# Post-norm spiking block and expert layer, one core: row sums from the producing instructions and squared deviations on ScalarE for two of the four norms

## The reference

```python
R, K, V = x @ Wr.T, x @ Wk.T, x @ Wv.T
# per time step:
r, k, v = lif(R_t), lif(K_t), lif(V_t)
h = h * 0.9 + k * v
y = r * h
x1 = layernorm(x + y @ Wo.T) * ln1_g + ln1_b
h2 = lif(x1 @ W1.T + b1) @ W2.T + b2
a  = layernorm(x1 + lif(h2)) * ln2_g + ln2_b
x3 = layernorm(x + a)                      # third norm, no gain or shift
# expert layer: softmax gates of 8 experts, the two largest, renormalised
out = layernorm(x3 + sum_e gate_e * (x3 @ We_e + be_e))   # last norm
```

## Time and profile before

| | |
|---|---|
| median of 3 runs | 991.33 us (990.92 to 992.54) |
| the profiled execution | 988.63 us, span of its core 986.8 us |
| mean granted clock of TensorE in it | 0.982 of full speed |
| PE busy, VectorE busy, ScalarE busy, GpSimd busy | 94%, 93%, 62%, 58% of the span |

### The profile page before, as it was taken

One profiled execution on the slowest core, in us unless ns is written; L12 is line 12 of the kernel. 1 busy time (PEld: TensorE's weight loads), 2 busy tenths in 40 slices (PEclk: granted clock), 3 DMA queues, 4 the chain that ended last, 5 costly groups with the idle time before them and its releaser, 6 DMA issues.

```text
span 986.8 us, 20602 instructions
## 1 busy us (share of the span) xinstructions
PE 925.7 (94%) x6506; PEld 859.1 (87%) x6506; DVE 915.6 (93%) x3682; ACT 611.8 (62%) x1389; POOL 571.8 (58%) x731
## 2 busy tenths in 40 slices
PE   5678789999999999999999999999999999999985
PEld 5578688999999999999999999999999999888764
DVE  6489998999999999999999999999999999988975
ACT  4565546666666676666666766667667666556452
POOL 1221113667676666666766666677766666765552
PEclk8799999999999999999999999999999999999999
DMA  8552222555554456555554555655545665456763
GB/s 259 129 108 66 42 54 55 118 119 118 108 112 107 100 122 119 119 122 107 114 107 99 119 118 120 127 111 104 113 97 114 119 127 110 97 97 118 141 127 86
DMA packets 59437, 109.71 MB, mean 111 GB/s; under 512 B 6592, under 2 KB 6592, under 8 KB 59328
## 3 DMA queue, kind: packets, MB, share of 16 engines
q0 software_dynamic: 37728, 68.71, 40.6%
q1 hardware_dynamic: 16992, 31.30, 9.7%
q10 hardware_dynamic: 4608, 8.39, 2.2%
HBM read 31.29 MB, written 8.39 MB: 40 GB/s over the span
## 4 chain that ended last, share of the span: by engine, by line
PE 73%; DVE 15%; ACT 3%; issue 3%; DMA 3%; POOL 2%; SPq 0%; POOLq 0%; ACTq 0%; DVEq 0%
PE ps_e L401 28%; PE ps_proj L401 12%; PE ps_proj L491 10%; PE ps_proj L476 10%; PE ps_proj L497 5%; PE ps_attn L401 3%; DVE U L887 3%; DVE V L894 2%; PE ps_zx L455 2%; DVE stats L966 2%; PE ps_attn L455 1%; DVE h L936 1%; DMA xt<-x_hi 1%; DMA xt<-x_T 1%; DMA acc<-term 1%
## 5 line engine op out<-in xcount | busy, mean ns | idle before, releaser
L887 DVE SCALAR_TENSOR_TENSOR U<-V,U 128x256 f32<-128x256 f32 (+4 forms) x576 | 227.7, 395 | 6.6 <-ACT U L658 2.9
L401 PE MATMUL ps_e<-we_hi,x_hi 128*128 128x512 f32 (+2 forms) x640 | 228.6, 357 | 3.6 <-DVE acc L1109 1.9
L894 DVE SCALAR_TENSOR_TENSOR V<-U 128x256 f32<-128x256 f32 (+4 forms) x576 | 224.2, 389 | 1.6
L401 PE MATMUL ps_e<-we_lo,x_hi 128*128 128x512 f32 (+2 forms) x640 | 223.3, 349 | 0.0
L401 PE MATMUL ps_e<-we_hi,x_lo 128*128 128x512 f32 (+2 forms) x640 | 222.7, 348 | 0.0
L1331 POOL TENSOR_SCALAR s<-U 128x256 fp32r<-128x256 f32 x208 | 192.1, 971 | 16.3 <-DVE V L894 16.3
L1317 POOL TENSOR_SCALAR veps<-mv 128x2 f32<-128x2 f32 x128 | 50.6, 396 | 256.6 <-DVE mv L972 254.4
L697 ACT ACTIVATE term<-ps_e,gate 128x256 f32<-128x256 f32 x372 | 160.3, 475 | 43.3 <-PE ps_e L401 43.3
L658 ACT ACTIVATE U<-ps_proj,cst 128x256 f32<-128x256 f32 x320 | 135.4, 480 | 70.5 <-PE ps_proj L497 64.1
L491 PE MATMUL ps_proj<-x_hi,w_hi 128*128 128x256 f32 x512 | 134.9, 284 | 3.1 <-ACT x_hi L676 1.7
L643 ACT ACTIVATE U<-ps_proj 128x512 f32<-128x512 f32 x96 | 57.6, 600 | 127.2 <-PE ps_proj L401 127.2
(11 more groups left out here) (108 smaller groups left out, 2302.3 us busy)
## 6 DMA issues: line engine op xcount, KB each, us to landing
acc<-term POOLq DMA_DIRECT2D x93, 256.0 KB, 3.7
odd_sum<-term POOLq DMA_DIRECT2D x93, 256.0 KB, 3.3
xt<-x_T SPq DMA_DIRECT2D x33, 256.0 KB, 2.9
xa<-x_tok SPq DMA_DIRECT2D x32, 256.0 KB, 3.2
xt<-x_hi POOLq DMA_DIRECT2D x32, 256.0 KB, 4.3
xb<-cst SPq DMA_DIRECT2D x32, 256.0 KB, 2.3
xb<-x_tok POOLq DMA_DIRECT2D x32, 256.0 KB, 6.1
out<-res ACTq DMA_DIRECT2D x31, 256.0 KB, 2.0
```

Of the source, the lines that this page charges most:

```text
L401: mm = pe.matmul(dst, lhs, rhs, start=(i == 0), stop=(i == n - 1))
L887: v.scalar_tensor_tensor(out=U[:, s, t, c0:c1], in0=V[:, c0:c1], scalar=0.5, in1=U[:, s, t, c0:c1], op0=ALU.mult, op1=ALU.add).then_inc(do ...
L894: v.scalar_tensor_tensor(out=V[:, c0:c1], in0=u, scalar=THRESHOLD, in1=u, op0=ALU.is_lt, op1=ALU.mult).then_inc(done, 1)
```

## The change

Norms 0 and 1 stay as they are. For norms 2 and 3 the instructions that make the norm's input also write its row sums (`accum_out`); the residual sum becomes two instructions, one for each tile. GpSimd turns the sums into minus the mean; ScalarE computes Square(x - mean) with its row sum, the result itself going to a tile that is free at that time; GpSimd makes variance + EPS and rstd of it; VectorE's shift is minus_mean * rstd. bn_stats and bn_aggr of both norms are gone, the slots of the shifts are unchanged.

```diff
@@ fin and norm counters
-        Y_STEPS, LN1_STEPS, LN2_STEPS, LN3_STEPS, GATE_STEPS, FIN_STEPS = 2, 6, 8, 5, 15, 7
+        Y_STEPS, LN1_STEPS, LN2_STEPS, LN3_STEPS, GATE_STEPS, FIN_STEPS = 2, 6, 8, 1, 15, 4
@@ ScalarE
+            def square(ln, src, junk):
+
+                for j in range(TILES):
+                    last = nc.scalar.activation(junk[:, j, :], src[:, j, :], ACT.Square, bias=minus_mean[ln][:, j:j + 1],
+                                                accum_out=squares[ln][:, j:j + 1])
+                last.then_inc(squares_ready[ln], 1)
+
+            def square_x3(b):
+                act.wait_ge(mean_ready[2], b.value(1, LAG_Z, 1))
+
+                if b.has(LAG_Y):
+                    act.wait_ge(x1T_done, b.value(1, LAG_Y, 1))
+                square(2, w, x1n)
+
+            def square_res(b):
+                act.wait_ge(mean_ready[3], b.value(1, LAG_F, 1))
+                square(3, res_of(b), odd_sum[:, b.slot(LAG_F, 2)])
...
                     for f in (0, 1):
                         to_lif(b, fill + f, COL_H1 + 2 * f * B, 2, C_B1 + 2 * f)
+                        if f == 0 and b.has(LAG_Z) and not b.early:
+                            square_x3(b)
...
                     to_lif(b, fill + 3, COL_H1 + 6 * B, 2, C_B1 + 6)
+                if b.has(LAG_F) and not b.late:
+                    square_res(b)
...
                             read_x3(b)
+                        if part == 5 and b.has(LAG_F) and b.late:
+                            square_res(b)
@@ VectorE
+                if ln in minus_mean:
+                    v.tensor_tensor(shift[ln][:], minus_mean[ln][:], rstd[ln][:], ALU.mult).then_inc(steps, 1)
+                    return
...
                 v.scalar_tensor_tensor(out=w[:, j, :], in0=w[:, j, :], scalar=rstd[1][:, j:j + 1],
-                                       in1=xb[:, j, :], op0=ALU.mult, op1=ALU.add).then_inc(ln2_steps, 1)
+                                       in1=xb[:, j, :], op0=ALU.mult, op1=ALU.add,
+                                       accum_out=sums[2][:, j:j + 1]).then_inc(ln2_steps, 1)
...
+                def total(other):
+
+                    for j in range(TILES):
+                        v.scalar_tensor_tensor(out=res_of(b)[:, j, :], in0=acc[:, b.slot(LAG_F, 2), j, :], scalar=1.0,
+                                               in1=other[:, j, :], op0=ALU.mult, op1=ALU.add,
+                                               accum_out=sums[3][:, j:j + 1]).then_inc(fin_steps, 1 + (j == 0 and b.k == LAST_BEAT))
...
-                    v.tensor_tensor(res[:], acc[:, b.slot(LAG_F, 2)], odd_sum[:, b.slot(LAG_F, 2)],
-                                    ALU.add).then_inc(fin_steps, 1)
-                if step == 2:
-                    chain(2)
-                    for j in range(TILES):
-                        bn_stats(3, j, res_of(b)[:, j, :], fin_steps)
-                if step == 3:
-                    if b.k == LAST_BEAT:
-                        dve.wait_ge(res_ready, b.value(1, LAG_F))
-                    bn_aggr(b, 3, fin_steps, FIN_STEPS, LAG_F, 4)
+                    total(odd_sum[:, b.slot(LAG_F, 2)])
...
-                    if slot == at["ln3_stats"]:
-                        after(ln2_steps, LN2_STEPS, LAG_Z, b, 8)
-                        bn_stats(2, 0, w[:, 0, :], ln3_steps)
-                        bn_stats(2, 1, w[:, 1, :], ln3_steps)
-                    if slot == at["ln3_aggr"]:
-                        bn_aggr(b, 2, ln3_steps, LN3_STEPS, LAG_Z, 2)
@@ GpSimd
+            def deviation(b, ln, steps, per, lag, done):
+
+                pool.wait_ge(steps, b.value(per, lag, done))
+                g.tensor_scalar(minus_mean[ln][:], sums[ln][:], -1.0 / D, None, ALU.mult).then_inc(mean_ready[ln], 1)
+                pool.wait_ge(squares_ready[ln], b.value(1, lag, 1))
+                g.tensor_scalar(veps[ln][:], squares[ln][:], 1.0 / D, EPS, ALU.mult, ALU.add).then_inc(rstd_ready[ln], 1)
+                pool.wait_ge(rstd_ready[ln], b.value(2, lag, 1))
+                g.tensor_tensor(rstd[ln][:], veps[ln][:], neg_half[:], ALU.pow).then_inc(rstd_ready[ln], 1)
...
-                    reciprocal_std(b, 2, ln3_steps, LN3_STEPS, LAG_Z, 4)
+                    deviation(b, 2, ln2_steps, LN2_STEPS, LAG_Z, LN2_STEPS)
...
-                    reciprocal_std(b, 3, fin_steps, FIN_STEPS, LAG_F, 6)
+                    deviation(b, 3, fin_steps, FIN_STEPS, LAG_F, FIN_STEPS - 1)
```

More of the change, by code:

```diff
@@ L246, in build @@
         gate_T = sb("gate_T", [STACK, TILES, P], F32R)
-        stats = [sb(f"stats{i}", [P, TILES, 6]) for i in range(4)]
-        mv = [sb(f"mv{i}", [P, TILES, 2]) for i in range(4)]
+        stats = [sb(f"stats{i}", [P, TILES, 6]) for i in range(2)]
+        mv = [sb(f"mv{i}", [P, TILES, 2]) for i in range(2)]
+        sums, minus_mean, squares = ({i: sb(f"{name}{i}", [P, TILES]) for i in (2, 3)} for name in ("sums", "minus_mean", "squares"))
         veps = [sb(f"veps{i}", [P, TILES]) for i in range(4)]
@@ L285, in build @@
         rstd_ready = [sem(f"rstd_ready{i}") for i in range(4)]
+        mean_ready, squares_ready = ({i: sem(f"{name}{i}") for i in (2, 3)} for name in ("mean_ready", "squares_ready"))
         e0_done, expert_done = sem("e0_done"), sem("expert_done")
@@ L791, in beat @@
                 if b.has(LAG_Z) and b.early:
-                    norm_x3(b)
+                    square_x3(b)
                 if b.ahead:
@@ L801, in beat @@
                     fill += 1
+                if b.has(LAG_Z) and b.early:
+                    norm_x3(b)
                 if b.has(LAG_Y) and not b.early:
@@ L817, in beat @@
                     read_x3(b)
+                if b.has(LAG_Z) and b.late:
+                    square_x3(b)
                 if b.has(LAG_M) and not b.early and not b.last_m:
@@ L857, in beat @@
                             read_x3(b)
+                        if part == 5 and b.has(LAG_F) and b.late:
+                            square_res(b)
+                if b.has(LAG_F) and (b.last_m or b.k == LAST_BEAT):
+                    square_res(b)
                 if b.has(LAG_F):
@@ L1116, in fin_stage @@
             def fin_stage(b, step):
-                chain = lambda n: after(fin_steps, FIN_STEPS, LAG_F, b, n)
                 if step == 0 and b.k == LAST_BEAT:
                     return
+                def total(other):
[3 more added lines that the diff above has]
+                                               accum_out=sums[3][:, j:j + 1]).then_inc(fin_steps, 1 + (j == 0 and b.k == LAST_BEAT))
                 if step == 1 and b.k == LAST_BEAT:
@@ L1122, in fin_stage @@
                     dve.wait_ge(term_ready, b.value(E - 1, LAG_F, E - 1))
-                    v.tensor_tensor(res_of(b)[:], acc[:, b.slot(LAG_F, 2)], bias_bank(b.k - 1)[:], ALU.add).then_inc(fin_steps, 2)
+                    total(bias_bank(b.k - 1))
                     return
```

## The result

The changed kernel takes **1032.97 us** (median of 4 runs, 1031.04 to 1035.13), the one before 991.31 (990.92 to 992.54): ratio 1.042, 95% interval 1.040 to 1.044. The profiled execution took 1032.87 us with a span of 1031.0, before 988.63 and 986.8. So 44.2 us of span have to be found.

What follows compares the result with a forecast made beforehand. PE was taken to set the steady beat, VectorE following with about half a microsecond of slack. 31.5 us steady plus 8 us drain, 39.5, on 991.33 gave 1030.5 us; range 1000 to 1050, the forecast's own 1012 to 1052.

Steps and rivals of the forecast that it cites:

- steady term: Steady beats: VectorE's wait for the shift makes each of 25 beats 1.26 us longer, 31.5 us in all.
- signs in the steady stretch: If right: PE 4 to 5% below 100%, VectorE near 90%, two shift waits of 1 to 2.5 us, x1_low not waiting.
- second rival: Slower by PE's banks alone: ScalarE reads late, PE waits 0.67 us per beat at an expert fill; 998 to 1012; chance 0.17.
- S, a pair of squares: ScalarE's two Square instructions with accumulator, 128x256 from SBUF: 0.99 us per pair, bounds 0.72 and 1.37.
- The accumulators on VectorE: VectorE's residual sum as two instructions, 0.79 us instead of 0.60, and 0.06 for each of four accumulator outputs.
- The new chain: Steady beats: GpSimd's operations and VectorE's last shift follow ScalarE's squares; shift 1.59 us later, beat 1.26 us longer.
- The fill: Two filling beats with a third norm: VectorE's 0.8 us partly spent in waits; 0 taken, bounds -1.5 and +1.
- The drain: Four drain beats: later shift, z_sum and x3 chain cost 1 to 2.8 us each; 8 us taken, bounds 3 and 11.
- The first rival: Faster: VectorE's wait doesn't come, PE keeps 28.06 us beats, less VectorE work shows only at the ends; 988.8 us; chance 0.15.
- The third rival: Much slower: one Square with accumulator near 1 us, a pair 1.9, loop 3.1 longer per beat; 1079 us; chance 0.08.

Runs made afterwards that it cites:

- e2: Kernel before, plus ScalarE's four squares in the steady beats at the change's places, results unused: 1012.7 us, ratio 1.022.
- e11: The changed kernel with GpSimd, in the drain's late beats, issuing two adding transfers ahead of its wait for the last norm's squares: 1028.1 us, ratio 1.035.
- e7: The changed kernel without ScalarE's squares, 1.0 standing in for both variances; sums, means, powers and shifts stay: 987.7 us, ratio 0.9945.
- e5: The changed kernel with VectorE's last-norm shift two slots later in steady beats, behind x3_low (slot 31 instead of 29): 1029.6 us, ratio 1.038.
- e9: e1 with GpSimd's issue of one transfer moved, in steady beats, between its veps and rstd of the last norm: 1031.3 us, ratio 1.039.
- e12: Kernel before, plus four idle squares per steady beat in front of ScalarE's third projection read, where it waited for PE anyway: 992.2 us, ratio 1.000.
- e1: The changed kernel with both norms' shifts made by GpSimd right behind its rstd instead of by VectorE: 1060.8 us, ratio 1.070.
- e6: e5 with ScalarE's last-norm squares moved, in steady beats, behind its read of x3 instead of ahead of expert part 3: 1056.8 us, ratio 1.064.

## Why the prediction was right, and where its sizes were off

**Direction, time and range held**: 1030.5 forecast, 1032.97 measured. That the time came so close is in part luck: the steady term was 6 us too large, the drain's 9.5 too small. Of its signs in the steady stretch, VectorE's two waits and the place of PE's (an expert fill) came as written, and x1_low waits no more. That PE's waits sit at the expert fills only it had named as a sign for its second rival. VectorE is at 91%, 1.1 us per beat less busy, as reckoned; PE's idle share is 1.1%, not 4 to 5, in a beat that is 3.6% longer. The rest doesn't show as idle time: products are 0.28 long and start 0.11 apart, so a short stall only uses up the overlap or makes a product longer, as in the PE row of e2 (0.39 us, where the same product was 0.28). Step by step:

- **S, a pair of squares**: 0.99 taken, 0.98 measured.
- **The accumulators on VectorE**: 0.79 + 0.12 taken for the residual sum, 0.70 measured (511.57 to 512.27). By the rule of the Trainium skill (VectorE: DVE Perf Modes, section Two Vector instructions with no wait between them) four more rows per beat should appear, and the trace agrees, DVE_READ_ACCUMULATOR, 0.08 us each; but behind the first of the pair the next instruction starts at 507.43, together with it, so in the queue they cost next to nothing.
- **The new chain**: the last shift was put 2 x 0.99 + 6.08 = 8.06 behind the first h1 read, and stands 7.79 behind it. The term that was too long is squares' end to shift, 1.49 against 1.25 (515.01 to 516.26). VectorE's stretch after it is 19.22, forecast 19.20. That makes a beat longer by 1.0 instead of 1.26: 25.3 us instead of 31.5.
- **The fill**: 0 taken, 1.4 measured in one pair of executions; kernels with one and the same fill differ by more (184.0 and 187.6), so 0 may well be right.
- **The drain**: 8 taken, bounds 3 and 11, 17.5 measured. This is the step that failed. It priced VectorE's own delay and z_sum behind it; it left out what is queued on GpSimd behind the wait for squares (e11: 5 to 7 us), and that PE's clock falls behind its longer waits (some 6 us, estimated at e11). It was hidden in the total because the steady term was too large by 6.2.
- **The first rival** (988.8): it could only decide if the squares took next to no time. e7 takes them away and gives back 4.9 us (992.6 to 987.7), where 2.5 was reckoned. The reason against this rival was right, its size half of what was measured.
- **The second rival** was set against the forecast as an alternative, at 0.67 per beat. It was not one: e2 shows its delay at 0.8 with VectorE's shifts out of it, and e5 and e9 show that without VectorE's waits for the shifts the beat is only 0.2 shorter. Both loops bind within 0.2 us of each other. The forecast named the loop that ended last, as the trace says, but "VectorE's wait costs 1 us per beat" would have been the wrong repair.
- **The third rival** had S at 1.9, which the trace excludes. A reload of tables didn't come either: the trace of the change holds one table load, at 0.73 us, and the squares stand right between the reads in every beat.

None of the kernels run keeps the squares' work real and beats the one before. The best place for them, by e12, is in front of the third projection read, and using it for real would mean to carry the residual into the next beat; that was not tried, and e7 bounds its gain at about 0.5%.

## What to carry to other kernels

Before moving work to an engine that is 62% busy, add up its idle time between the point where it is last released and the read that another engine waits for, not over the span: 1.96 us in a stretch with 1.0 us of slack cost 21 us, and the same 1.96 us elsewhere in the beat cost nothing. An idle copy of the moved work, at the place it will stand, measures this without building the change. And when a wait is the last to end, look for what would be last without it; here it stood 0.2 us behind.

## What the runs showed of the hardware that was not expected

- **Accumulator output.** On ScalarE it is a row of its own, ACTIVATION_READ_ACCUMULATOR, 0.20 us long and 0.09 in the queue; on VectorE DVE_READ_ACCUMULATOR, 0.08 long and beside the next instruction.
- **A transfer issued by GpSimd right into its compares** goes with slower steps on both engines: VectorE's steps 0.62 instead of 0.41 us, the eight compares 8.2 instead of 7.4, the beat 1.1 to 1.3 longer. So it is in one beat each of e2, e5 and e7 and in all steady beats of e1, and e9, which moves the issue, gives 30 us back. That the order on GpSimd is the cause is shown; that the issue itself does it is not: with it e9 puts the rstd and the shift between the issue and the compares, and in e6, where the issue also runs into them, they take 7.33 us while VectorE's steps of h are the long ones.
- **A lower granted clock behind idle stretches of PE**, 0.55 and 0.69 in 5 us windows of the drain, makes a late chain later: products 0.23 us apart at full clock stand up to 0.43 apart there. So some of the drain's loss, 6 us by the estimate at e11, would be a second effect of the same waits; no run separates the two.
